# A mixture-of-experts loop on one core: pairs written out on TensorE, slot transposes between the two tiles, activated tiles copied in halves

## The chip, the cores and the metric

The kernel runs on one core of one Trainium2 chip. The metric is the device time of one execution in microseconds (us); the number that counts is the median of several executions. The core has TensorE (matrix products, transposes and the loading of their weights), VectorE, ScalarE, GpSimd and SyncE, each with its own stream of instructions; semaphores order them. PSUM is the memory into which TensorE writes, in eight banks of 512 float32 columns; SBUF is the working memory.

## The reference

A small network of six blocks on x, which is 2 x 1024 rows of 256 floats:

```python
x = x + 0.5 * moe(layernorm(x))          # 16 experts, 2 per row
x = x + attention(layernorm(x))
x = x + 0.5 * moe(layernorm(x))
x = x + 0.5 * lora(layernorm(x))         # 8 low-rank experts
x = x + latent_attention(layernorm(x))
x = x + 0.5 * lora(layernorm(x))

# moe: combine holds the softmax of the two largest router logits of a row
for e in range(NUM_EXPERTS):             # 16
    h = silu(x @ W1[e]) @ W2[e]          # 256 -> 512 -> 256
    out = out + combine[:, e:e + 1] * h
```

All is float32. The change touches the two moe blocks alone.

## The kernel before

`moe_stage` runs twice, once for each moe block. Its first part normalizes the rows, computes the router, chooses two experts for each row and sorts the 4096 pairs of row and expert by expert into tiles of 128 slots. There are at most 47 tiles (`NTILE`), each with one expert; the number of the expert of each is in `EI` in SBUF. The second part, which the change is about, takes the tiles two by two (23 pairs, `NPAIR`, and one last tile). `u` is 0 or 1, the place of a tile in its pair; every buffer has two halves, one for each.

For a tile, GpSimd gathers its 128 rows from memory into `XS` (line 675). TensorE transposes them into bank u (`slots_t`, 630, two transposes), VectorE copies that to `ST` (525). TensorE multiplies with the expert's `W1` into bank 2 + u (`hidden`, 637: two products of 512 columns, which the trace shows as four, each with its weight load). ScalarE applies silu, bank 2 + u to `HS` (552). TensorE transposes `HS` into bank 4 + u (`hidden_t`, 644, four transposes), VectorE copies the bank of 512 columns to `HT` (521). TensorE multiplies with the expert's `W2` into bank 6 + u (`expert_out`, 651: four products of 256 columns, in the trace eight). ScalarE copies the result to `YS` (556), GpSimd scatters it to memory (691).

The order on each engine is the order of the code. For pair i TensorE's is: read two expert numbers from `EI` into registers (657), `hidden` of tile 0 and 1, `hidden_t` of tile 0 and 1, `slots_t` for both tiles of the next pair, `expert_out` of tile 0 and 1. VectorE's: the two `HT` copies, the two `ST` copies. GpSimd's: two gathers, each released by a slot transpose, then two scatters, each released by a `YS` copy, then the wait for their landing (692, 693). TensorE, VectorE and ScalarE run the pairs in a loop with a register as counter (`Fori`; TensorE's at 656); the last tile, number 46, is written out behind it (666 to 669, 526 to 528, 557 to 562).

The semaphores named in the change: `s_thp` counts transposed tiles in PSUM, `s_thc` the copies of them, `s_hs` activated tiles, `s_tap` and `s_tac` transposed slots and their copies, `s_y` and `s_yc` results in PSUM and their copies. `at(n)` is the value after n of them. A wait belongs to the engine's sequencer: it holds the instructions behind it, while those already handed over go on.

Of the kernel before, what the change touches and what calls it, by code (L numbers as in the profile page):

```python
# [28 lines left out]
P = 128  # L29
# [7 lines left out]
NE, FF, TOP = 16, 512, 2  # L37
KF = FF // P

NTILE = 47  # L40
assert NTILE == NT * TOP + NE - 1
NPAIR = NTILE // 2
# [241 lines left out]
def moe_stage(nc, g, dram, rep):  # L284
# [6 lines left out]
    S = lambda name, each, **kind: g.sem("moe_" + name, each, rep, **kind)  # L291
# [12 lines left out]
    s_xs = [S(f"slots_loaded{u}", 16 * (NSLOT // 2), pool_dma=True) for u in range(2)]  # L304
    s_tap, s_tac = S("slotsT_in_psum", NSLOT), S("slotsT_copied", NSLOT)
    s_h, s_hs = S("hidden_in_psum", NTILE), S("hidden", NTILE)
    s_thp, s_thc = S("hiddenT_in_psum", NTILE), S("hiddenT_copied", NTILE)
    s_y, s_yc = S("expert_out_in_psum", NTILE), S("expert_out_copied", NTILE)
    s_yd = S("expert_out_stored", 16 * NTILE, pool_dma=True)
    s_yf = S("expert_out_free", NPAIR + 1)  # L310
# [5 lines left out]
    with ExitStack() as ctx:  # L316
# [27 lines left out]
        EC, EI = sb("EC", [1, NSLOT]), sb("EI", [1, NSLOT], I32)  # L344
# [9 lines left out]
        HT = sb("HT", [P, 2, KF, P])  # L354
        YS = sb("YS", [P, 2, D])
        bank = g.bank
# [4 lines left out]
        with nc.Block(no_gpsimd_drain=True) as block:  # L361
# [11 lines left out]
            def _(dve):  # L373
# [140 lines left out]
                for u in range(2):  # L514
                    dve.wait_ge(s_tap.handle, s_tap.at(u + 1))
                    dve.tensor_copy(ST[:, u], bank(u)[:, 0:KD * P].rearrange("p (k s) -> p k s", s=P)).then_inc(s_tac.handle, 1)  # L516
                with dve.Fori(0, NPAIR) as i:
                    for u in range(2):
                        dve.wait_ge(s_thp.handle, s_thp.at(2 * i + u + 1))
                        dve.wait_ge(s_y.handle, s_y.at(2 * i))  # L520
                        dve.tensor_copy(HT[:, u], bank(4 + u)[:, :].rearrange("p (k s) -> p k s", s=P)).then_inc(s_thc.handle, 1)  # L521
                    for u in range(2):
                        dve.wait_ge(s_tap.handle, s_tap.at(2 * i + u + 3))
                        dve.wait_ge(s_h.handle, s_h.at(2 * i + u + 1))
                        dve.tensor_copy(ST[:, u], bank(u)[:, 0:KD * P].rearrange("p (k s) -> p k s", s=P)).then_inc(s_tac.handle, 1)
                dve.wait_ge(s_thp.handle, s_thp.at(NTILE))
                dve.wait_ge(s_y.handle, s_y.at(NTILE - 1))
                dve.tensor_copy(HT[:, 0], bank(4)[:, :].rearrange("p (k s) -> p k s", s=P)).then_inc(s_thc.handle, 1)  # L528

            @block.scalar  # L530
            def _(act):
# [33 lines left out]
            def _(pe):  # L565
# [61 lines left out]
                def slots_t(u, j, loads):  # L627
                    pe.wait_ge(s_xs[u].handle, s_xs[u].at(16 * loads))
                    for k in range(KD):
                        ins = pe.transpose(bank(u)[:, k * P:(k + 1) * P], XS[:, u, k * P:(k + 1) * P], ident)  # L630
                    ins.then_inc(s_tap.handle, 1)

                def hidden(u, expert, done, j):
                    pe.wait_ge(s_tac.handle, s_tac.at(j + 1))
                    pe.wait_ge(s_hs.handle, s_hs.at(done))
                    for k in range(KD):
                        ins = pe.matmul(bank(2 + u)[:, :], ST[:, u, k, :], g.W1[:, expert, k, :], start=(k == 0), stop=(k == KD - 1))  # L637
                    ins.then_inc(s_h.handle, 1)

                def hidden_t(u, done, j):  # L640
                    pe.wait_ge(s_hs.handle, s_hs.at(j + 1))
                    pe.wait_ge(s_thc.handle, s_thc.at(done))
                    for k in range(KF):
                        ins = pe.transpose(bank(4 + u)[:, k * P:(k + 1) * P], HS[:, u, k * P:(k + 1) * P], ident)  # L644
                    ins.then_inc(s_thp.handle, 1)

                def expert_out(u, expert, done, j):
                    pe.wait_ge(s_thc.handle, s_thc.at(j + 1))
                    pe.wait_ge(s_yc.handle, s_yc.at(done))
                    for k in range(KF):  # L650
                        ins = pe.matmul(bank(6 + u)[:, 0:D], HT[:, u, k, :], W2[:, expert, k, :], start=(k == 0), stop=(k == KF - 1))  # L651
                    ins.then_inc(s_y.handle, 1)

                slots_t(0, 0, 1)
                slots_t(1, 1, 1)
                with pe.Fori(0, NPAIR) as i:
                    experts = [pe.value_load(EI[0:1, bass.ds(2 * i + u, 1)], min_val=0, max_val=NE - 1) for u in range(2)]
                    for u in range(2):
                        hidden(u, experts[u], 2 * i, 2 * i + u)
                    for u in range(2):  # L660
                        hidden_t(u, 2 * i, 2 * i + u)
                    for u in range(2):
                        slots_t(u, 2 * i + u + 2, i + 2)
                    for u in range(2):
                        expert_out(u, experts[u], 2 * i, 2 * i + u)
                expert = pe.value_load(EI[0:1, NTILE - 1:NTILE], min_val=0, max_val=NE - 1)
                hidden(0, expert, NTILE - 1, NTILE - 1)
                hidden_t(0, NTILE - 1, NTILE - 1)
                expert_out(0, expert, NTILE - 1, NTILE - 1)

            @block.gpsimd
            def _(pool):
# [1837 lines left out]
```

## Time and profile before

| | us |
|---|---|
| median of 3 runs | 2213.99 (2212.3 to 2214.46) |
| the profiled execution | 2221.23 |
| its span, from the first to the last instruction | 2219.5 |
| expert loop of the first moe block, pairs 1 to 22 | 190.72, from 81.12 |
| expert loop of the second moe block, pairs 1 to 22 | 190.71, from 797.83 |
| busy in the span: TensorE products | 1996.0 (90%) |
| VectorE | 1276.7 (58%) |
| ScalarE | 817.4 (37%) |
| GpSimd | 867.5 (39%) |

In the views PE is a product or transpose of TensorE and PEld its weight load, which runs beside the product before; DVE is VectorE, ACT ScalarE, POOL GpSimd, SP SyncE. L644 is line 644. "x4" behind a row is a number of instructions taken together, and the time ahead of it then reaches from the start of the first to the end of the last. A product's shown duration is longer than the distance at which products follow each other, since they are pipelined. In square brackets stand the idle time of the engine before the row and what ended it; "issue" means that the profile shows nothing that it waited for. A name with q (PEldq) is the engine's sequencer, which waits, branches and reads registers and is not counted as busy. [...]

### The profile page before, as it was taken

How to read it: one execution, taken by the hardware profiler on the slowest of the kernel's cores; microseconds unless marked ns; L12 is line 12 of the kernel's file. 1: busy time of each engine (PE TensorE's matmuls, PEld its weight loads, DVE VectorE, ACT ScalarE, POOL GpSimd, SP SyncE). 2: the span in 40 equal slices, each digit the busy share in tenths (PEclk: the TensorE clock that was granted, in tenths of full speed). 3: DMA queues.
4: the chain of work that ended last, by engine and by line, in shares of the span. 5: the costliest groups of instructions: out<-in, count | busy, mean ns of one | idle time of the engine just before them, and what ended most of it. 6: DMA issues, size and time to landing. Idle time of an engine off the chain costs nothing. (4 is left out here: it accounts for less than half of the span.)

```text
span 2219.5 us, 29901 instructions
## 1 busy us (share of the span) xinstructions
PE 1996.0 (90%) x8700; PEld 1249.6 (56%) x8701; DVE 1276.7 (58%) x2970; ACT 817.4 (37%) x1549; POOL 867.5 (39%) x684
## 2 busy tenths in 40 slices
PE   5899958898888789986779999999999999999987
PEld 5566635455554756654545555555566555555556
DVE  6322275777775722216656666666656666667525
ACT  2122244554555212223324444444523444444423
POOL 0344311231112034441115556555424555665631
PEclk9999968999899689996769999999999999999999
DMA  9111232232220811124141122222032222212101
GB/s 385 48 58 63 55 126 29 29 44 43 29 29 1 341 52 63 57 54 179 21 95 45 47 57 57 57 57 57 12 75 54 56 58 57 50 44 50 31 1 51
DMA packets 60570, 150.63 MB, mean 68 GB/s; under 512 B 12976, under 2 KB 18304, under 8 KB 58176
## 3 DMA queue, kind: packets, MB, share of 16 engines
q1 hardware_dynamic: 50208, 120.43, 20.6%
q0 software_dynamic: 9120, 24.92, 3.6%
q10 hardware_dynamic: 1152, 4.19, 0.5%
q8 instruction: 43, 0.70, 0.1%
q14 instruction: 47, 0.39, 0.1%
HBM read 68.95 MB, written 18.61 MB: 39 GB/s over the span
## 5 line engine op out<-in xcount | busy, mean ns | idle before, releaser
L1834 POOL TENSOR_TENSOR mla_PS<-mla_PS,mla_PT 128x1024 f32<-128x1024 f32 x192 | 458.4, 2388 | 200.2 <-ACT mla_PT L2120 198.8
L2263 DVE TENSOR_REDUCE mla_MXP<-PS 128x1 f32<-128x512 f32 x512 | 334.4, 687 | 199.7 <-PE PS L1915 197.5
L2120 ACT ACTIVATE mla_PT<-PS 128x512 f32<-128x512 f32 x512 | 293.5, 599 | 421.0 <-PE PS L1935 375.4
L1944 PE MATMUL PS<-mla_PT,mla_CN 128*64 128x512 f32 x1024 | 274.2, 614 | 0.0
L521 DVE COPY moe_HT<-PS 128x512 f32<-128x512 f32 x92 | 63.7, 692 | 307.0 <-PE PS L644 301.2
L1915 PE MATMUL PS<-mla_KH,mla_QH 113*128 113x512 f32 x512 | 199.2, 456 | 18.0 <-DMA mla_KL<-mla_SL 17.8
L675 POOL DMA_INDIRECT moe_XS<-rows_in,moe_GI x96 | 93.7, 976 | 307.5 <-PE PS L630 171.3
L1935 PE MATMUL PS<-mla_QH,mla_KH 113*128 113x512 f32 x512 | 210.3, 411 | 1.7 <-ACT mla_QH L2104 1.5
L1935 PE MATMUL PS<-mla_QL,mla_KH 113*128 113x512 f32 x512 | 201.8, 394 | 0.0
L1935 PE MATMUL PS<-mla_QH,mla_KL 113*128 113x512 f32 x512 | 201.7, 394 | 0.0
L1140 ACT ACTIVATE att_PT<-PS 128x1024 f32<-128x1024 f32 (+1 forms) x192 | 152.3, 812 | 95.2 <-PE PS L975 93.4
L1915 PEld LDWEIGHTS PS<-mla_KH,mla_QH 113*128 113x128 f32 x512 | 91.2, 194 | 168.0 <-DVE mla_MXP L2263 89.7
L637 PE MATMUL PS<-W,moe_ST 128*128 x376 | 174.4, 607 | 2.7 <-DVE moe_ST L516 2.7
L1834 POOL TENSOR_TENSOR mla_PS<-mla_PT 128x1024 f32<-128x1024 f32 x32 | 76.3, 2384 | 248.1 <-ACT mla_PT L2120 248.1
L651 PE MATMUL PS<-W,moe_HT 128*128 x752 | 170.4, 379 | 1.7 <-DVE moe_HT L528 1.7
L954 PE MATMUL PS<-att_KT,att_QT 128*128 128x512 f32 (+3 forms) x384 | 145.8, 424 | 24.4 <-DVE att_MX L1251 10.1
L651 PEld LDWEIGHTS PS<-W,moe_HT 128*128 128x128 f32 x752 | 139.1, 190 | 19.1 <-issue 2.1
L1249 DVE CUSTOM_DVE_ANT_0 PS<-PS,att_SEEN 128x128 f32<-128x128 f32 (+3 forms) x256 | 122.8, 508 | 45.8 <-PE PS L954 43.7
L852 POOL TENSOR_SCALAR_AFFINE_SELECT att_PT<-att_PT 128x256 f32<-128x256 f32 x128 | 52.2, 409 | 242.4 <-ACT att_PT L1140 242.3
L2275 DVE RECIPROCAL PS<-PS 128x128 f32<-128x128 f32 x128 | 108.7, 918 | 52.4 <-PE PS L1951 52.4
L1935 PEld LDWEIGHTS PS<-mla_QH,mla_KH 113*128 113x128 f32 x512 | 96.4, 188 | 68.3 <-issue 22.0
L954 PEld LDWEIGHTS PS<-att_KT,att_QT 128*128 128x128 f32 x384 | 74.8, 210 | 102.3 <-DVE att_MX L1251 38.5
(297 smaller groups left out, 3192.4 us busy)
## 6 DMA issues: line engine op xcount, KB each, us to landing
W<-in_W_dram SPq DMA_DIRECT2D x16, 2048.0 KB, 28.0
mla_QH<-mla_SH SPq DMA_DIRECT2D x64, 128.0 KB, 2.4
mla_KH<-mla_SH SPq DMA_DIRECT2D x64, 128.0 KB, 2.4
mla_QL<-mla_SL SPq DMA_DIRECT2D x64, 128.0 KB, 2.5
mla_KL<-mla_SL SPq DMA_DIRECT2D x64, 128.0 KB, 2.4
mla_KH<-mla_SH SPq DMA_DIRECT2D x64, 96.0 KB, 2.4
mla_KL<-mla_SL SPq DMA_DIRECT2D x64, 96.0 KB, 2.4
sums_Y<-rows_out SPq DMA_DIRECT2D x9, 512.0 KB, 6.0
```

The lines of the kernel that those rows point to most:

```text
L637: ins = pe.matmul(bank(2 + u)[:, :], ST[:, u, k, :], g.W1[:, expert, k, :], start=(k == 0), stop=(k == KD - 1))
L651: ins = pe.matmul(bank(6 + u)[:, 0:D], HT[:, u, k, :], W2[:, expert, k, :], start=(k == 0), stop=(k == KF - 1))
L954: ins = pe.matmul(out[:, m, :], QT[:, H % 2, h, i * P:(i + 1) * P], KT[:, H % 2, h // 2, k0:k0 + w], start=(m == 0), stop=(m == len(hs) - 1))
L1140: act.activation(PT[:, kk % 2, 2 * pair:2 * pair + 2, c0:HB], st_banks(s)[:, :, c0:HB], ACT.Exp, scale=SEQ ** -0.5).then_inc(s_p.handle, 1)
L1249: ins = dve.tensor_tensor_reduce(part, part, seen, 1.0, LEAST, ALU.mult, ALU.max, MX[:, q, c, h, t:t + 1])
L1834: pool.tensor_tensor(PS[:, :], PT[:, slot(0), :] if k == 1 else PS[:, :], PT[:, slot(k), :], ALU.add).then_inc(s_ps.handle, 1)
L1915: pe.matmul(bank(piece_bank(n))[:, :], QH[USED, buf, h, tile * P:(tile + 1) * P], KH[USED, buf, h, c * HB:(c + 1) * HB], start=True, stop= ...
L1935: ins = pe.matmul(bank(st_bank(s, h))[:, :], kk[USED, buf, h, ks], qq[USED, buf, h, qs], start=(n == 0), stop=(n == 2))
L1944: ins = pe.matmul(bank(6)[h * DKVL:(h + 1) * DKVL, :], CN[:, b, k, 0:DKVL], PT[:, slot(k), h * HB:(h + 1) * HB], start=(k == 0), stop=(k = ...
L2120: act.activation(PT[:, slot(k), h * HB:(h + 1) * HB], bank(st_bank(s, h))[:, :], ACT.Exp, scale=MLA_SCALE).then_inc(s_p.handle, 1)
L2263: dve.tensor_reduce(MXP[:, n // NPC, c, h, t:t + 1], bank(piece_bank(n))[:, :], AX_X, ALU.max).then_inc(s_mx.handle, 1)
L2275: dve.reciprocal(bank(A)[:, cols], bank(A)[:, cols]).then_inc(s_rc.handle, 1)
```

## The change

On VectorE the copy of an activated, transposed tile (512 columns) becomes two copies of 256 columns, each of which counts in `s_thc`, so that this semaphore now counts to 94. The order within a pair becomes: copies of tile 0, the two slot copies, copies of tile 1. On TensorE the pairs are written out in Python and no longer run in a loop. The expert numbers of the next pair are read behind `hidden` of this one, those of the first pair where they were. `slots_t` of both tiles now stands between `hidden_t` of tile 0 and `hidden_t` of tile 1. `expert_out` waits for the first half copy ahead of its first chunk and for the second ahead of its third.

```diff
--- before.py
+++ after.py
@@ -304,7 +304,7 @@
     s_xs = [S(f"slots_loaded{u}", 16 * (NSLOT // 2), pool_dma=True) for u in range(2)]
     s_tap, s_tac = S("slotsT_in_psum", NSLOT), S("slotsT_copied", NSLOT)
     s_h, s_hs = S("hidden_in_psum", NTILE), S("hidden", NTILE)
-    s_thp, s_thc = S("hiddenT_in_psum", NTILE), S("hiddenT_copied", NTILE)
+    s_thp, s_thc = S("hiddenT_in_psum", NTILE), S("hiddenT_copied", 2 * NTILE)
     s_y, s_yc = S("expert_out_in_psum", NTILE), S("expert_out_copied", NTILE)
     s_yd = S("expert_out_stored", 16 * NTILE, pool_dma=True)
     s_yf = S("expert_out_free", NPAIR + 1)
@@ -514,18 +514,22 @@
                 for u in range(2):
                     dve.wait_ge(s_tap.handle, s_tap.at(u + 1))
                     dve.tensor_copy(ST[:, u], bank(u)[:, 0:KD * P].rearrange("p (k s) -> p k s", s=P)).then_inc(s_tac.handle, 1)
+                def hidden_copy(u, done, j):
+                    dve.wait_ge(s_thp.handle, s_thp.at(j + 1))
+                    dve.wait_ge(s_y.handle, s_y.at(done))
+                    for half in range(2):
+                        part = bank(4 + u)[:, half * HALF:(half + 1) * HALF]
+                        dve.tensor_copy(HT[:, u, half * KF // 2:(half + 1) * KF // 2], part.rearrange("p (k s) -> p k s", s=P)).then_inc(s_thc.handle, 1)
+
+                HALF = KF // 2 * P
                 with dve.Fori(0, NPAIR) as i:
-                    for u in range(2):
-                        dve.wait_ge(s_thp.handle, s_thp.at(2 * i + u + 1))
-                        dve.wait_ge(s_y.handle, s_y.at(2 * i))
-                        dve.tensor_copy(HT[:, u], bank(4 + u)[:, :].rearrange("p (k s) -> p k s", s=P)).then_inc(s_thc.handle, 1)
+                    hidden_copy(0, 2 * i, 2 * i)
                     for u in range(2):
                         dve.wait_ge(s_tap.handle, s_tap.at(2 * i + u + 3))
                         dve.wait_ge(s_h.handle, s_h.at(2 * i + u + 1))
                         dve.tensor_copy(ST[:, u], bank(u)[:, 0:KD * P].rearrange("p (k s) -> p k s", s=P)).then_inc(s_tac.handle, 1)
-                dve.wait_ge(s_thp.handle, s_thp.at(NTILE))
-                dve.wait_ge(s_y.handle, s_y.at(NTILE - 1))
-                dve.tensor_copy(HT[:, 0], bank(4)[:, :].rearrange("p (k s) -> p k s", s=P)).then_inc(s_thc.handle, 1)
+                    hidden_copy(1, 2 * i, 2 * i + 1)
+                hidden_copy(0, NTILE - 1, NTILE - 1)
 
             @block.scalar
             def _(act):
@@ -639,34 +643,39 @@
 
                 def hidden_t(u, done, j):
                     pe.wait_ge(s_hs.handle, s_hs.at(j + 1))
-                    pe.wait_ge(s_thc.handle, s_thc.at(done))
+                    pe.wait_ge(s_thc.handle, s_thc.at(2 * done))
                     for k in range(KF):
                         ins = pe.transpose(bank(4 + u)[:, k * P:(k + 1) * P], HS[:, u, k * P:(k + 1) * P], ident)
                     ins.then_inc(s_thp.handle, 1)
 
                 def expert_out(u, expert, done, j):
-                    pe.wait_ge(s_thc.handle, s_thc.at(j + 1))
                     pe.wait_ge(s_yc.handle, s_yc.at(done))
                     for k in range(KF):
+                        if k % (KF // 2) == 0:
+                            pe.wait_ge(s_thc.handle, s_thc.at(2 * j + 1 + k // (KF // 2)))
                         ins = pe.matmul(bank(6 + u)[:, 0:D], HT[:, u, k, :], W2[:, expert, k, :], start=(k == 0), stop=(k == KF - 1))
                     ins.then_inc(s_y.handle, 1)
 
                 slots_t(0, 0, 1)
                 slots_t(1, 1, 1)
-                with pe.Fori(0, NPAIR) as i:
-                    experts = [pe.value_load(EI[0:1, bass.ds(2 * i + u, 1)], min_val=0, max_val=NE - 1) for u in range(2)]
+                def expert_of(j):
+                    return pe.value_load(EI[0:1, j:j + 1], min_val=0, max_val=NE - 1)
+
+                experts = [expert_of(u) for u in range(2)]
+                for i in range(NPAIR):
                     for u in range(2):
                         hidden(u, experts[u], 2 * i, 2 * i + u)
-                    for u in range(2):
-                        hidden_t(u, 2 * i, 2 * i + u)
+                    later = [expert_of(j) for j in range(2 * i + 2, min(2 * i + 4, NTILE))]
+                    hidden_t(0, 2 * i, 2 * i)
                     for u in range(2):
                         slots_t(u, 2 * i + u + 2, i + 2)
+                    hidden_t(1, 2 * i, 2 * i + 1)
                     for u in range(2):
                         expert_out(u, experts[u], 2 * i, 2 * i + u)
-                expert = pe.value_load(EI[0:1, NTILE - 1:NTILE], min_val=0, max_val=NE - 1)
-                hidden(0, expert, NTILE - 1, NTILE - 1)
+                    experts = later
+                hidden(0, experts[0], NTILE - 1, NTILE - 1)
                 hidden_t(0, NTILE - 1, NTILE - 1)
-                expert_out(0, expert, NTILE - 1, NTILE - 1)
+                expert_out(0, experts[0], NTILE - 1, NTILE - 1)
 
             @block.gpsimd
             def _(pool):
```

## Rows read from the trace of the kernel before

**Rows 1.** The page: its head and part 1.
```profile
span 2219.5 us, 29901 instructions
...
PE 1996.0 (90%) x8700; PEld 1249.6 (56%) x8701; DVE 1276.7 (58%) x2970; ACT 817.4 (37%) x1549; POOL 867.5 (39%) x684
```

**Rows 2.** Windows over pairs 1 to 22 of both stages: busy us of each engine.
```profile
81.12:271.84 190.72, 185.20 (x794) 127.73 (x793) 45.00 (x88) 42.67 (x88) 85.30 (x87) 1.00 0.20 60
797.83:988.54 190.71, 185.21 (x793) 127.73 (x792) 45.00 (x88) 42.67 (x88) 85.30 (x87) 1.00 0.19 60
```

**Rows 3.** Timeline of one pair: start, duration, engine, line, what, count, idle before.
```profile
185.15 3.60 PE L637 MATMUL PS<-W,moe_ST 128*128 x8
...
187.15 0.60 ACT L552 ACTIVATE moe_HS<-PS 128x512 f32<-128x512 f32 x1 [1.42 <-PE PS L637]
...
188.58 0.60 PE L644 MATMUL PS<-C,moe_HS 128*128 128x128 f32 x4
...
188.78 0.60 ACT L552 ACTIVATE moe_HS<-PS 128x512 f32<-128x512 f32 x1 [1.04 <-PE PS L637]
189.31 1.51 DVE L521 COPY moe_HT<-PS 128x512 f32<-128x512 f32 x2 [6.50 <-PE PS L644]
189.43 0.42 PEld L644 LDWEIGHTS PS<-C,moe_HS 128*128 128x128 f32 x4 [0.49 <-ACT moe_HS L552]
189.44 0.66 PE L644 MATMUL PS<-C,moe_HS 128*128 128x128 f32 x4 [0.25 <-ACT moe_HS L552]
...
189.93 0.60 PE L630 MATMUL PS<-C,moe_XS 128*128 128x128 f32 x4
...
190.36 3.62 PE L651 MATMUL PS<-W,moe_HT 128*128 x16
190.58 0.99 POOL L675 DMA_INDIRECT moe_XS<-rows_in,moe_GI  x1 [3.60 <-PE PS L630]
190.74 0.75 DVE L525 COPY moe_ST<-PS 128x256 f32<-128x256 f32 x2
...
193.82 3.60 PE L637 MATMUL PS<-W,moe_ST 128*128 x8
```

**Rows 4.** Waits of 80 to 270 us: us in total, times, longest.
```profile
PEld PS L644 <- ACT moe_HS L552: 10.8, 22, 0.5
```

**Rows 5.** Lines 675 (gathers), 691 (scatters) and 693 (wait for landing, 180 to 200 us).
```profile
DMA to landing us min/median/max: 2.6/2.8/4.5
...
DMA to landing us min/median/max: 2.4/2.4/3.6
...
L693 POOLq EVENT_SEMAPHORE  x2: 17/17/17, 188.4 to 197.1; - x2
```

**Rows 6.** Timeline of the first stage's last tile, where TensorE stands idle.
```profile
275.10 0.69 DVE L528 COPY moe_HT<-PS 128x512 f32<-128x512 f32 x1 [5.60 <-PE PS L644]
275.89 0.51 PEld L651 LDWEIGHTS PS<-W,moe_HT 128*128 128x128 f32 x3 [1.07 <-issue]
275.92 0.67 PE L651 MATMUL PS<-W,moe_HT 128*128 x2 [0.86 <-DVE moe_HT L528]
```

**Rows 7.** Copies of lines 521 and 525: ns least, median, most, first and last start.
```profile
L521 DVE COPY moe_HT<-PS x92: 691/692/693, 76.6 to 984.9; 128x512 f32<-128x512 f32 x92
...
L525 DVE COPY moe_ST<-PS x92: 411/415/416, 78.0 to 985.8; 128x256 f32<-128x256 f32 x92
```

**Rows 8.** TensorE's sequencer around that pair, lines 656 (whole stage), 657 and 642.
```profile
L656 PEldq COMPARE_BRANCH  x46: 83/215/238, 78.9 to 986.1; - x46
...
L657 PEldq TENSOR_LOAD <-moe_EI x2: 298/300/302, 183.2 to 183.9; - x2
L657 PEldq SEQ_ASSERT  x2: 18/18/18, 183.8 to 184.5; - x2
...
L642 PEldq EVENT_SEMAPHORE  x2: 51/51/51, 185.5 to 187.8; - x2
```

**Rows 9.** Timeline of the first stage's first pair.
```profile
68.45 0.42 DVE L516 COPY moe_ST<-PS 128x256 f32<-128x256 f32 x1 [0.73 <-PE PS L630]
...
69.87 0.50 PEld L637 LDWEIGHTS PS<-W,moe_ST 128*128 128x128 f32 x2 [1.86 <-issue]
```

**Rows 10.** The page's part 3, and the waits of the whole span.
```profile
q8 instruction: 43, 0.70, 0.1%
...
PEld PS L954 <- issue: 18.2, 31, 0.8
```

## The prediction

> **What bounds the kernel now.** I read four views, from coarse to fine. The page gives the span, 2219.5 us, and TensorE busy for 90% of it [rows 1]. [...]
>
> The timeline of one pair then shows where TensorE waits [rows 3]. Its own work is the two `hidden` groups (185.15 to 188.58), four transposes of tile 0's activations, four of tile 1's, four slot transposes, and sixteen products (190.36 to 193.82). The next pair starts when those sixteen have been issued: 16 x 0.216 = 3.46 us after 190.36, so nothing is lost at the loop's end. Four transposes take 0.43 us of issue (189.93 to 190.36). From 188.58 to 190.36 there are twelve, 1.30 us of work in 1.78 us. The missing 0.48 us lies between tile 0's transposes, issued by 188.58 + 0.43 = 189.02, and tile 1's, whose weight load starts at 189.43. The row names the releaser: the activation of tile 1 on ScalarE, 188.78 + 0.60 = 189.38. The waits view repeats it for all 22 pairs, 10.8 us on the weight-load side, 0.49 us each, and names nothing else that holds TensorE [rows 4].
>
> **The slot transposes between the tiles.** Now TensorE issues tile 0's transposes (188.58), then the slot transposes, then tile 1's. The first eight end at 188.58 + 2 x 0.43 = 189.45. Tile 1's activation still ends at 189.38, and its first weight load still starts at 189.43, as now. In stream a load starts 0.11 us before its transpose's turn, which would be 189.34, so this one is late by 0.09 and its transpose keeps the 0.06 us by which it is long now (0.66 us for four in rows 3, where four in stream take 0.60). It counts from 189.49, the four are issued by 189.93, and the products may begin there instead of at 190.36: 0.43 us gained a pair, and 0.04 us of the wait is left.
>
> Two things are moved past. The slot transposes come 0.91 us earlier than now, and they need the gathers. Gather tile 0 starts at 190.58 and lands a median of 2.8 us later [rows 5], at 193.4; its transposes stand at about 197 in the next pair, so 3 us of cover remain. On GpSimd the order is unchanged: two gathers, two scatters, a wait for their landing. That wait ends at 197.1, the gathers are released about 199.25 (190.58 + 8.67) [rows 3, 5]. With the change the gathers start at about 189.67 and the next ones 8.24 later, at 197.9; the landing moves with the products to about 196.7. 1.2 us are left where 2.15 were, enough.
>
> **The copy in halves.** This is what could take the gain away again. Products of tile 0 need its transposed activations in SBUF. The whole copy runs from 189.31 to 190.00. Then TensorE's sequencer must see it: after the last tile, where TensorE stands idle, the copy ends at 275.10 + 0.69 = 275.79 and the weight load starts at 275.89 [rows 6], 0.10 us later. Its first two products take 0.67 us, where 0.216 + 0.38 = 0.60 is the pace in stream, so they count from 275.92 + 0.08 = 276.00, 0.11 us after the load's start. So a whole copy would allow the first product at 190.00 + 0.21 = 190.21, and of the 0.43 us only 0.15 would be gained. The copy is cut into two of 256 columns each. No such copy of the hidden activations is in the trace; the nearest row is the slot copy, also PSUM to SBUF, 128x256: 0.415 us against 0.692 for 128x512 [rows 7]. The first half then ends at 189.31 + 0.415 = 189.725, the weight load may start at 189.83, the first product at 189.94. Against 189.93 from TensorE's own stream that costs 0.01 us: the two limits meet almost exactly. Bounds: none (0) to the whole copy's (0.28 us); I take 0.01 because the slot copy has the same shape, source and engine.
>
> The second half ends 0.33 us after the first (two slot copies take 0.75 in all, rows 3), at 190.06. The third chunk's product, which needs it, stands at 189.94 + 4 x 0.216 = 190.80. Behind it VectorE has the two slot copies (190.0 to 190.7) and then tile 1's halves, about 190.65 to 191.4. Tile 1's products need the first one (ready at 191.05) at 189.94 + 8 x 0.216 = 191.67: 0.6 us of cover, less 0.2 for the hand-over. The new order on VectorE, with tile 1's copy behind the slot copies, therefore costs nothing; the slot copies are needed at 193.4 only.
>
> [...]
>
> **Pairs written out, expert numbers read ahead.** Now a pair ends with a compare-and-branch (0.215 us on the sequencer) and two reads of expert numbers with their register work, first at 183.2 and done by 184.5 [rows 8]. All that lies under the sixteen products before 185.15, since the sequencer runs ahead of the array, so removing it gains 0 a pair. The reads now come after `hidden`. The sequencer is done with issuing it at 185.5 (the wait of L642) and passes the activation's wait at 187.8 [rows 8]: 2.3 us of cover for 1.3 us of reads. If that cover were gone, up to 1.3 us a pair. At the start of a stage the reads still follow the slot transposes; the slot copies are done at 68.45 + 0.42 = 68.87 and `hidden` starts at 69.87 [rows 9]. Without the loop's set-up and index arithmetic I put this 0 to 0.4 us earlier, take 0.25.
>
> **The last tile.** Everything in it is serial, and the first half copy is ready 0.692 - 0.415 = 0.28 us sooner than the whole one [rows 6, 7]. Gained: 0.28 us a stage. What follows (the last scatter, its landing, the sums) is serial too and moves with it.
>
> **The sum.** A pair gains 190.36 - 189.94 = 0.42 us, or 0.43 with the rounded starts the other way; I take 0.43. There are 23 intervals from the first `hidden` of a stage to the last tile's: 23 x 0.43 = 9.9; plus 0.28 and 0.25: 10.4 a stage, 20.9 for both. The profiled execution took 2221.23 us (span 2219.5 and 1.7 around it), 0.3% above the median of 2213.99; the gain is a matter of fixed steps, so it is taken off both: 2200.3 for a profiled run, and **2213.99 - 20.9 = 2193.1 us** for the median, 0.94% faster. A pair would last 8.24 us.
>
> **The rivals.** (a) *The half copy becomes the bound.* The two limits meet within 0.01 us, so any 0.1 us in the hand-over (a register step ahead of the weight load, a longer half copy) shows in full. With the first product 0.1 to 0.28 us late a pair gains 0.15 to 0.33: 0.33 gives 16 us (2198), 0.15 gives 8 us (2206). For it: no margin. Against it: both durations are rows. (b) *The gap isn't filled*, because slot transposes are held by something the present order hides (a gather): same time within 0.2%, about 2213. Against it: 3 us of cover. [...]
>
> **How the numbers follow.** The forecast, 0.82: by the bounds of its parts a pair gains 0.38 to 0.46 and both ends 0.3 to 0.7 a stage, 18 to 22.5 us, so 2191.5 to 2196. Rival (a) 0.12, 2196 to 2206; (b) 0.02; (c) 0.04, above 2218. With some 1.5 us for the median itself (runs went from 2212.3 to 2214.46) the range is 2190 to 2199: it reaches into (a) up to a gain of 15 us and leaves out its lower half, (b) and (c). Faster by over 0.2%: 0.82 + 0.12 = 0.94; within: 0.02; slower: 0.04.
>
> **What would show it.** A pair of 8.24 us at clock 1.00 in both loops; no idle time over 0.1 us before tile 1's weight load; the slot transposes right behind tile 0's; half copies of 0.42 us, the first ending about 0.2 us before the first product; first product 1.35 us after the pair's first transpose, now 1.78. Wrong if the products wait for the half copy (a), if idle time shows every three pairs or so (c), or if the first transposes of a pair come later than 3.43 us after its start (the reads).

## The result, and the profile after

| | before | after |
|---|---|---|
| median, us | 2213.05 | 2201.91 |
| lowest to highest of 12 runs, us | 2209.83 to 2215.53 | 2196.72 to 2208.44 |
| profiled execution, us | 2221.23 | 2202.58 |
| its span and mean granted clock | 2219.5, 0.939 | 2200.8, 0.939 |
| length of a pair, us | 8.669 | 8.348 |

The ratio is 0.9946, with an interval of 0.9936 to 0.9956: the changed kernel is faster by 0.54%, or 11.1 us in the medians (the kernel before was timed again beside it, so its median differs from the one shown ahead of the prediction). The forecast was 2193.1 us, a gain of 20.9, with a range of 2190 to 2199. The sign was right, the size half of what was said, and the time lies outside the range.

The page's head and its part 1 answer to rows 1, the row of queue 8 to rows 10. Queue 8 has 17 fetches more than before.

```profile
span 2200.8 us, 29601 instructions
...
PE 1992.3 (91%) x8700; PEld 1251.4 (57%) x8700; DVE 1277.8 (58%) x3064; ACT 817.6 (37%) x1549; POOL 866.3 (39%) x684
...
q8 instruction: 60, 0.98, 0.2%
```

The windows over pairs 1 to 22 of both stages (start:end and length, then busy us with the count of instructions in the order PE, PEld, DVE, ACT, POOL, then PEclk, which is TensorE's granted clock as a share of full speed, DMA share and GB/s; rows 2 of before):

```profile
81.22:264.87 183.65, 183.65 (x793) 128.32 (x792) 45.80 (x132) 42.70 (x88) 84.49 (x87) 1.00 0.20 62
790.80:974.46 183.66, 183.66 (x794) 128.32 (x793) 45.79 (x132) 42.69 (x88) 84.51 (x87) 1.00 0.20 63
```

183.65 / 22 = 8.348 us a pair, against 190.72 / 22 = 8.669 before, at the same granted clock (1.00 in all four windows), where 8.24 was forecast. Each of these 44 pairs lasts 8.346 to 8.349 us, so nothing happens now and then: each loses the same. TensorE counts as busy all the time, although it isn't at its pace: the product that waits is shown with 0.454 us instead of 0.379 (in stream they follow each other at 3.46 / 16 = 0.216 us, rows 3). The number to read is the length. The timeline of one pair shows the loss (rows 3 of before):

```profile
189.74 3.60 PE L641 MATMUL PS<-W,moe_ST 128*128 x8
...
193.17 0.60 PE L648 MATMUL PS<-C,moe_HS 128*128 128x128 f32 x4
193.37 0.60 ACT L556 ACTIVATE moe_HS<-PS 128x512 f32<-128x512 f32 x1 [1.04 <-PE PS L641]
193.50 0.47 PEld L634 LDWEIGHTS PS<-C,moe_XS 128*128 128x128 f32 x4
193.61 0.60 PE L634 MATMUL PS<-C,moe_XS 128*128 128x128 f32 x4
193.90 0.76 DVE L522 COPY moe_HT<-PS 128x256 f32<-128x256 f32 x2 [6.26 <-PE PS L648]
194.02 0.42 PEld L648 LDWEIGHTS PS<-C,moe_HS 128*128 128x128 f32 x4
194.04 0.63 PE L648 MATMUL PS<-C,moe_HS 128*128 128x128 f32 x4
194.27 0.99 POOL L684 DMA_INDIRECT moe_XS<-rows_in,moe_GI  x1 [2.69 <-PE PS L634]
194.53 3.32 PEld L656 LDWEIGHTS PS<-W,moe_HT 128*128 128x128 f32 x16
194.56 3.69 PE L656 MATMUL PS<-W,moe_HT 128*128 x16
194.57 0.75 DVE L530 COPY moe_ST<-PS 128x256 f32<-128x256 f32 x2
195.23 0.75 DVE L522 COPY moe_HT<-PS 128x256 f32<-128x256 f32 x2
...
197.87 0.41 PEld L641 LDWEIGHTS PS<-W,moe_ST 128*128 128x128 f32 x2
```

The order is the new one: tile 0's transposes (193.17), the slot transposes (193.61), tile 1's (194.04), with no gap between them. (Tile 1's activation still ends last by a little: 193.37 + 0.60 = 193.97, and the load of its transposes starts at 194.02, which puts them some 0.04 us behind their turn, as forecast.) The next pair starts 8.35 us after this one, at 198.09. The wait for tile 1's activation, 10.8 us in rows 4, is gone; what the waits view keeps of it is the last tile, 1.5 us once. The copy of tile 0 now comes in two halves in 0.76 us.

What remains is the start of the products. Their loads begin at 194.53. The rows of their line, and of the wait ahead of it, say why (the window is 194.2 to 194.7 us; durations are ns least, median, most, then the first and the last start; PEldq is TensorE's sequencer; the copies' row is of the whole kernel):

```profile
L522 DVE COPY moe_HT<-PS x188: 414/416/426, 77.0 to 978.1; 128x256 f32<-128x256 f32 x188
...
L655 PEldq EVENT_SEMAPHORE  x1: 51/51/51, 194.4 to 194.4; - x1
...
L656 PEldq ALU_OP  x1: 32/32/32, 194.5 to 194.5; - x1
...
L656 PE MATMUL PS<-W,moe_HT x1: 454/454/454, 194.6 to 194.6; 128*128 x1
```

The first half copy starts at 193.90 and takes 0.425 us: the 48 half copies that VectorE starts after idling take 0.424 to 0.426 us, the other 140 take 0.414 to 0.417. It ends at 194.32. The sequencer's wait on line 655 is over at 194.36, then a second instruction follows on line 656 at 194.47 (in the raw trace; the row rounds it to 194.5), and only then the load, at 194.53. The raw trace also names the semaphores: the instruction of line 655 waits for `s_thc`, the one of line 656 for `s_yc`, whose copies were done at 190.31. From the copy's end to the load it is 0.205 us, where the prediction put 0.10 by rows 6. The transposes' own stream would allow the first product at 193.17 + 1.30 + 0.05 = 194.52, where the 0.05 is mostly what tile 1's activation still costs. Counted back from its end at the pace in stream the product starts at 194.63: 0.11 us late. From the copy's end to the load it is 0.204 to 0.205 us in 45 of the 46 pairs, and 0.213 in the very first. (8.348 - 8.242) x 46 = 4.9 us; the 8.242 is measured below.

### The profile page after: what moved, and what is told of

It reads as the page before. It is cut to its first block and busy times, and to the rows that moved or that the text cites. A ratio compares the mean times of both kernels' runs of the same rounds, so it can differ in the third digit from the quotient of the medians.

```text
span 2200.8 us, 29601 instructions
## 1 busy us (share of the span) xinstructions
PE 1992.3 (91%) x8700; PEld 1251.4 (57%) x8700; DVE 1277.8 (58%) x3064; ACT 817.6 (37%) x1549; POOL 866.3 (39%) x684
## 3 DMA queue, kind: packets, MB, share of 16 engines
q1 hardware_dynamic: 50208, 120.43, 20.9%
## 5 line engine op out<-in xcount | busy, mean ns | idle before, releaser
L522 DVE COPY moe_HT<-PS 128x256 f32<-128x256 f32 x188 | 70.7, 418 | 301.5 <-PE PS L648 301.5
```

## The experiments

All kernels that follow are the changed one with the one edit shown, or the kernel before with it. Each ratio is against runs of the kernel before on the same chip.

**1. The changed kernel again.** No edit.

> The changed kernel itself, once more, beside the others on the same chip. In its profile a pair lasts 8.348 us (0.321 us less than before), which over 2 x 23 intervals is 14.8 us, and the heads and tails of the two stages give 1 us more: 15.8. The medians of the first measurement gave 11 to 12. If the missing 4 us are chance of that measurement, this one gives 14 to 17; if they are real and lie in the stages that the change doesn't touch, it gives 11 to 12 again.

Measured: 2200.92 us, ratio 0.9952 (0.9935 to 0.9968), and 8.349 us a pair. The gain is 10 to 11 us on another chip too.

**2. The two waits ahead of the products swapped.**

```diff
 def expert_out(u, expert, done, j):
-    pe.wait_ge(s_yc.handle, s_yc.at(done))
     for k in range(KF):
         if k % (KF // 2) == 0:
             pe.wait_ge(s_thc.handle, s_thc.at(2 * j + 1 + k // (KF // 2)))
+            if k == 0:
+                pe.wait_ge(s_yc.handle, s_yc.at(done))
```

> Theory: the first product of tile 0 is late because the wait for the half copy is followed by a second waiting instruction (the wait for the copied results), 0.106 us behind it on TensorE's sequencer, and by the order in which the code has them. With the two waits in the other order, the half copy's is the last and only one instruction stands between it and the weight load. Expected: first weight load of the products 0.10 to 0.11 us after the half copy's end (now 0.205), a pair of 8.24 to 8.25 us, 4.6 to 5 us less than the changed kernel in all. Rival: the half copy itself, 0.425 us and not 0.415, or the release of TensorE by VectorE takes that long whatever stands behind it: then the pair stays at 8.35 us.

Measured: 2195.20 us, ratio 0.9924 (0.9904 to 0.9945). The windows over pairs 1 to 22, the timeline of one pair, and the sequencer's rows of lines 656 and 657 in it:

```profile
80.11:261.43 181.32, 181.32 (x794) 127.90 (x792) 45.76 (x132) 42.66 (x88) 84.54 (x87) 1.00 0.20 63
```

```profile
174.20 0.60 PE L648 MATMUL PS<-C,moe_HS 128*128 128x128 f32 x4
...
174.93 0.76 DVE L522 COPY moe_HT<-PS 128x256 f32<-128x256 f32 x2 [6.16 <-PE PS L648]
175.05 0.42 PEld L648 LDWEIGHTS PS<-C,moe_HS 128*128 128x128 f32 x4
...
175.45 0.30 PEld L657 LDWEIGHTS PS<-W,moe_HT 128*128 128x128 f32 x2
```

```profile
L656 PEldq EVENT_SEMAPHORE  x1: 51/51/51, 175.1 to 175.1; - x1
...
L657 PEldq ALU_OP  x1: 32/32/32, 175.4 to 175.4; - x1
```

181.32 / 22 = 8.242 us. The half copy starts 0.73 us after the pair's first transpose as before, and ends at 175.35; the load starts at 175.45, 0.10 us later instead of 0.205, and is right behind the transposes' loads. Nothing but the order of two waits differs. In the program as written the changed kernel waits for `s_yc` first; in what TensorE runs, the wait written first comes last, on the instruction just ahead of the load, and the other on an instruction of its own before it. `s_yc` (the products of the pair before, copied out) has been reached long before (at 190.31 in the changed kernel, where the copy ends at 194.32). With `s_thc` on the earlier instruction, a wait that is already satisfied stands between the one that comes last and the load, and costs 0.106 us a pair. Swapped, the satisfied one is passed first (175.06 in the raw trace), while TensorE still works, and the one for `s_thc` (175.39) stands next to the load. The raw traces show this reversal in all the kernels compared here, the loop of the kernel before included (its source has `s_thc` first; what TensorE runs has `s_yc` at 189.56 us and `s_thc` at 190.04), but not in the loops of experiments 4 and 8. These have `s_yc` first in the source too, yet it sits on a register operation of line 655 and `s_thc` on one of line 656, next to the load, which starts 0.10 us after the copy; in the last tile of the same two kernels, which is written out, it is 0.21 us. So the order in the source alone doesn't say on which instruction a wait ends up.

**3. The pairs written out and nothing else**, in the kernel before: the loop over pairs becomes Python's, and the reads go behind `hidden`.

```diff
-with pe.Fori(0, NPAIR) as i:
-    experts = [pe.value_load(EI[0:1, bass.ds(2 * i + u, 1)], ...) for u in range(2)]
+experts = [expert_of(u) for u in range(2)]
+for i in range(NPAIR):
     for u in range(2):
         hidden(u, experts[u], 2 * i, 2 * i + u)
+    later = [expert_of(j) for j in range(2 * i + 2, min(2 * i + 4, NTILE))]
```

> The kernel before with one part of the change: pairs written out on TensorE and expert numbers read behind hidden; order and whole copies as before. By my sum a pair keeps its 8.669 us and each stage starts 0.35 to 0.4 us sooner: 2212 to 2213, ratio 0.9995 to 1.0. Rival: written-out instructions cost something outside the loops' pace (fetches, what follows the stage): then it is up to 4 us slower than before, and that is where the missing 4 us of the change went.

Measured: 2215.08 us, ratio 1.0012 (0.9998 to 1.0025), with these windows:

```profile
80.09:270.81 190.72, 185.19 (x794) 127.72 (x793) 45.00 (x88) 42.64 (x88) 85.05 (x87) 1.00 0.19 61
```

190.72 us for 22 pairs, to the hundredth what rows 2 have. By itself this part is worth nothing in the pairs. Queue 8 has 60 fetches here too, 8 of them in 81 to 271 us, where the kernel before has none; they lengthen none of these pairs.

**4. The loop kept, all else changed.**

```diff
-experts = [expert_of(u) for u in range(2)]
-for i in range(NPAIR):
+with pe.Fori(0, NPAIR) as i:
+    experts = [pe.value_load(EI[0:1, bass.ds(2 * i + u, 1)], ...) for u in range(2)]
```

> The changed kernel with TensorE's loop kept (and its reads at the head of each pair): slot transposes between the tiles and half copies only. By the sequencer's lead in the trace of before, the reads are hidden, and a pair lasts 8.35 us as in the changed kernel, perhaps up to 0.1 more since the sequencer has the reads and the branch to do ahead of the next pair. Against before: 14.8 us and the tails' 0.3, 15 us. Rival: if writing out the pairs costs 4 us outside the loops, this kernel is 3 to 4 us faster than the changed one; if it is needed for the gain, its pair is longer than 8.45 us.

Measured: 2218.99 us, ratio 1.0039 (1.0027 to 1.0052): slower than the kernel before, where a pair of 8.35 us had been expected. The windows, the timeline around a pair's end, and the rows of the sequencer there (line 656 in 183.9 to 184.4 us, line 662 in the window after it):

```profile
80.48:274.45 193.97, 186.93 (x792) 126.27 (x793) 45.78 (x132) 42.34 (x87) 84.53 (x86) 1.00 0.19 58
799.47:992.44 192.97, 186.93 (x793) 126.28 (x794) 45.78 (x132) 42.39 (x88) 84.53 (x86) 1.00 0.19 59
```

```profile
182.50 3.32 PEld L656 LDWEIGHTS PS<-W,moe_HT 128*128 128x128 f32 x16
182.60 3.63 PE L656 MATMUL PS<-W,moe_HT 128*128 x16
182.65 0.75 DVE L530 COPY moe_ST<-PS 128x256 f32<-128x256 f32 x2
183.31 0.75 DVE L522 COPY moe_HT<-PS 128x256 f32<-128x256 f32 x2
...
186.55 0.30 PEld L641 LDWEIGHTS PS<-W,moe_ST 128*128 128x128 f32 x2 [0.73 <-issue]
```

```profile
L656 PEldq ALU_OP  x1: 32/32/32, 184.1 to 184.1; - x1
...
L662 PEldq TENSOR_LOAD <-moe_EI x2: 298/299/300, 184.9 to 185.6; - x2
L662 PEldq SEQ_ASSERT  x2: 18/18/18, 185.4 to 186.2; - x2
```

193.97 / 22 = 8.817 us a pair in the first stage and 192.97 / 22 = 8.771 in the second, 0.15 and 0.10 longer than before. The sequencer can't run ahead further than the wait for tile 1's second half copy, which stands before the last two products. That copy ends at 183.31 + 0.75 = 184.06, and the wait is over at 184.10. Then come the last products' issue, the branch (0.21 us) and the two reads (0.30 us each) with their register work, done at 186.2, and the next pair's load at 186.55, 2.45 us after the wait, with 14 instructions of the sequencer in between. In experiment 2, where nothing holds it, this load starts 3.25 us after the first product (175.55 to 178.80), here that would be 182.60 + 3.25 = 185.85. It is 0.70 us late, of which 0.10 comes back because it needn't wait for its turn (from it to the next transposes it is 3.54 us instead of 3.64). The hand-over to the first product is 0.10 us in this kernel (the copy ends at 182.40, the load starts at 182.50), so 8.24 is what it starts from: 8.24 + 0.60 = 8.84, the length of this pair. The others of the first stage last 8.83 to 8.86 us and those of the second 8.79 to 8.80; the last interval of each stage, which ends with one read instead of two and no branch back, lasts 8.34.

**5. The kernel before, as the one under test.** No edit: what the comparison gives for no change.

> The kernel before, run as if it were a variant, beside the others and with a profile of its own. Four variants so far came out some 5 us later, against the kernel before, than their expert stages explain: the traces give 15.6, 21, 2 and -2.6 us for these stages, the medians gave 10.6, 16.3, -3.6 and -7.5. If that is real and lies in the untouched stages, this run gives a ratio of 1.000. If it comes from how the kernel before is run among the others, it gives 1.002 (5 us) for the same code. Its profile shows whether the attention and latent-attention stages last 435 and 1132 us, as in the variants, or less.

Measured: 2214.21 us, ratio 1.0003 (0.9991 to 1.0014), 8.669 us a pair.

**6. The copy left whole**, in the changed kernel.

```diff
-for half in range(2):
-    part = bank(4 + u)[:, half * HALF:(half + 1) * HALF]
-    dve.tensor_copy(HT[:, u, half * KF // 2:(half + 1) * KF // 2], part.rearrange(...)).then_inc(s_thc.handle, 1)
+dve.tensor_copy(HT[:, u], bank(4 + u)[:, :].rearrange(...)).then_inc(s_thc.handle, 1)
```

With it `s_thc` counts to 47 again, and `expert_out` waits for it once, behind `s_yc` in the source as in the changed kernel.

> The changed kernel with the activated tile copied whole (512 columns), everything else as changed. By the prediction's sum the first product then starts 0.692 + 0.205 us after the copy's start, 0.27 us later than in the changed kernel, where the half copy takes 0.425: a pair of 8.62 us, some 12 us slower than the changed kernel in all. Rival: if the copy isn't what the first product waits for, the pair stays at 8.35 us.

Measured: 2214.31 us, ratio 1.0002 (0.9991 to 1.0012), with these windows:

```profile
81.29:270.81 189.52, 186.35 (x793) 128.32 (x792) 42.92 (x88) 42.69 (x88) 84.48 (x87) 1.00 0.19 60
```

189.52 / 22 = 8.615 us, where 8.62 had been expected. Without the halves the new order on TensorE is worth 0.054 us a pair, and nothing that the median shows. The halves carry 0.27 of the 0.32 us.

**7. The best of what the runs point to:** the waits swapped as in 2, and the first pair's expert numbers read ahead of the first slot transposes, so that TensorE waits with them for a gather that it has to wait for anyway.

```diff
-slots_t(0, 0, 1)
-slots_t(1, 1, 1)
 def expert_of(j):
     return pe.value_load(EI[0:1, j:j + 1], min_val=0, max_val=NE - 1)
 experts = [expert_of(u) for u in range(2)]
+slots_t(0, 0, 1)
+slots_t(1, 1, 1)
```

> The changed kernel with the two waits swapped, and with the first pair's expert numbers read ahead of the first slot transposes instead of behind them. A pair of 8.242 us as with the waits swapped alone. The reads take 1.3 to 1.6 us of TensorE's sequencer where it waits for a gather anyway, so each stage's first hidden follows its slot copies after 0.2 us instead of 0.6 to 0.9: about 1 us in all less than with the waits swapped. Against before: the expert stages give 22 us; with the 4 to 5 us that all variants so far lost elsewhere, 17 to 18 us in the medians.

Measured: 2191.61 us, ratio 0.9901 (0.9885 to 0.9917). It beats both kernels: 22 us less than the one before beside it, where the changed one was 11 us less. Its windows, and the first stage's first pair:

```profile
77.92:259.24 181.32, 181.32 (x793) 127.91 (x792) 45.75 (x132) 42.66 (x88) 84.56 (x87) 1.00 0.20 63
```

```profile
67.48 0.42 DVE L516 COPY moe_ST<-PS 128x256 f32<-128x256 f32 x1 [0.92 <-PE PS L634]
...
68.14 0.55 PEld L641 LDWEIGHTS PS<-W,moe_ST 128*128 128x128 f32 x2
...
68.60 0.42 DVE L516 COPY moe_ST<-PS 128x256 f32<-128x256 f32 x1 [0.69 <-PE PS L634]
```

The copy at 67.48 is that of tile 0's slots, the only one that tile 0's `hidden` needs. It ends at 67.91, and `hidden` loads 0.24 us later, right behind tile 1's slot transposes; tile 1's copy starts only at 68.60. The same copy in the kernel before, and in the changed kernel with the first load of `hidden`:

```profile
67.29 0.42 DVE L516 COPY moe_ST<-PS 128x256 f32<-128x256 f32 x1 [0.89 <-PE PS L630]
```

```profile
68.01 0.42 DVE L516 COPY moe_ST<-PS 128x256 f32<-128x256 f32 x1 [0.93 <-PE PS L634]
...
70.16 0.50 PEld L641 LDWEIGHTS PS<-W,moe_ST 128*128 128x128 f32 x2 [1.44 <-issue]
```

From the copy's end to the load it was 69.87 - 67.71 = 2.16 us before (the load is in rows 9), and it is 70.16 - 68.44 = 1.72 us in the changed kernel: the loop's set-up is gone, the two reads are still there. Rows 9 show tile 1's copy, which ends at 68.87; it is not what `hidden` waited for, the reads are.

The edit is worth more than the 1 us that was expected. Against experiment 2 the two stages are 1.9 and 2.4 us shorter: 1.2 and 1.0 between the first gather and the first `hidden`, and 0.7 and 1.5 in the first interval, which lasts 9.56 and 9.84 us here and 10.27 and 11.31 there. The first interval of the same code varies by up to 0.75 us from trace to trace (the last section), so that second part may be luck in part. By the medians the kernel gains 22 us, where 17 to 18 were expected.

**8. The loop kept, and VectorE's order of before:** kernel 4 with both tiles' half copies ahead of the slot copies.

```diff
-hidden_copy(0, 2 * i, 2 * i)
+for u in range(2):
+    hidden_copy(u, 2 * i, 2 * i + u)
 for u in range(2):
     ...
-hidden_copy(1, 2 * i, 2 * i + 1)
```

> TensorE's loop kept, slot transposes between the tiles, half copies, but on VectorE the order of before: both tiles' activated copies, then the slot copies. Theory: with the loop kept and the new order on VectorE a pair took 8.84 us because the wait for tile 1's second half copy (over at 184.06 us of that trace) holds the sequencer, and behind it still stand the branch and both reads (2.4 us) before hidden can be issued, 0.49 us too late. In the old order tile 1's copies end 0.46 us sooner, so hidden is 0 to 0.05 us late: a pair of 8.24 to 8.29 us, as good as written out. Rival: the branch and the reads cost 0.5 us a pair in themselves, once the gap between the tiles no longer absorbs them: then the pair stays at 8.7 to 8.85 us.

Measured: 2198.34 us, ratio 0.9938 (0.9922 to 0.9954), with these windows, the sequencer's row of line 656 (169.1 to 169.5 us), and the load of the pair after it:

```profile
80.10:263.50 183.40, 183.40 (x794) 126.26 (x793) 47.82 (x132) 42.67 (x88) 84.45 (x87) 1.00 0.19 62
```

```profile
L656 PEldq ALU_OP  x1: 32/32/32, 169.3 to 169.3; - x1
```

```profile
171.79 0.30 PEld L641 LDWEIGHTS PS<-W,moe_ST 128*128 128x128 f32 x2 [0.23 <-issue]
```

183.40 / 22 = 8.336 us, and 8.345 in the second stage, between the expectation (8.24 to 8.29) and the rival. From the wait for the last half copy to the next pair's load it is 2.45 us again (169.34 to 171.79), but the wait is over sooner, and the load comes 0.20 us late instead of 0.70; with 0.10 of it regained, 8.24 + 0.10 = 8.34. Experiments 3, 4 and 8 together: taking the branch out and moving the reads behind `hidden` gains 0.00 us a pair in the kernel before, and what they cost at a pair's end in the other two, where the sequencer takes 2.45 us from the last wait to the next load, goes with where VectorE's last half copy ends. The written-out pairs are needed above all by the new order on VectorE, where the loop costs 0.55 to 0.60 us a pair. With VectorE's old order it still costs 0.09 to 0.10 (8.336 and 8.345 against 8.242), about what the order of the waits costs the changed kernel. Written-out pairs with VectorE's old order weren't run.

**9. The kernel before with 48 satisfied waits** put on TensorE at the start of each stage, where it stands idle for a gather: does a mere shift of the code change the rest?

```diff
 pe.wait_ge(s_ei.handle, s_ei.at(1))
+for _ in range(48):
+    pe.wait_ge(s_ei.handle, s_ei.at(1))
```

> The kernel before with 48 waits that are satisfied already (2.4 us of TensorE's sequencer) where TensorE waits for the first gather, in both stages. A pair keeps 8.669 us. All later instructions of TensorE stand 48 instructions further on for each stage, which is what all variants have in common. If the 4 to 5 us that they lost come from where TensorE's instructions lie, this kernel is 3 to 5 us slower than before too; if not, the ratio is 1.000 within 0.1%.

Measured: 2215.63 us, ratio 1.0012 (0.9999 to 1.0026), 8.669 us a pair.

**10. The kernel before once more**, beside 9.

> The kernel before as a variant once more, on the chip of the three others: its ratio says how much of a difference of 1 to 2 us means nothing. Expected 1.000 within 0.1%. Its trace is the third of before: the latent-attention stage took 1137.7 and 1137.2 us in the first two and 1131.6 to 1134.8 in four of the five variants, although the medians say that before is the one with less time there.

Measured: 2215.09 us, ratio 1.0011 (1.0001 to 1.0022). So 9 shows nothing that no edit at all doesn't show, and neither does 3. A ratio of 1.001 is not a difference here, even where its interval leaves out 1.

## Why the prediction went wrong, point by point

**What bounds the kernel, the wait that goes, the slot transposes: right.** The twelve transposes stand in stream, the wait for the activation is gone and no gather holds the slot transposes (the gather at 194.27 here starts 0.06 us after they end). Once the wait order is mended a pair lasts 8.242 us, where 8.24 was said.

**The failed step: the hand-over to the first product, put at 0.10 us by rows 6.** It measured 0.205 in the changed kernel and 0.10 in experiments 2, 4 and 8. The row was right for what it shows: there the order in the source was `s_thc`, then `s_yc`, so the copy's wait sat on the instruction next to the load. The diff turns this order round in `expert_out`, and the prediction took no account of it. The half copy also took 0.425 us instead of 0.415. With a margin of 0.01 us the hand-over shows in full: 0.321 a pair instead of 0.43. Swapping the waits gives 0.106 of the missing 0.109 back, which leaves 0.003 for the longer half copy and all else. 46 x 0.109 = 5.0 us of the 9.8 that are missing in the median; another 0.5 us is missing at the ends of the stages and 4.3 us outside them, as the passages below work out. It is rival (a), and its condition was named (a register step ahead of the weight load), but at 0.12 it was given too little: where two limits meet within 0.01 us, a forecast by either one needs every instruction between them to be counted, and I counted none.

**The whole copy: right in kind, mis-sized by the same term.** 0.15 us of gain were to remain by the hand-over of 0.10; experiment 6 has 0.054. It too has the waits in the new order, and its load starts 0.205 us after the copy's end, 0.105 later than was put: 0.15 - 0.105 = 0.045. The whole copy with the waits swapped wasn't run.

**The half copies: 0.415 us by the row of the slot copies, right within 0.011.** All 188 half copies take 0.414 to 0.426 us. A second instruction has a price of its own: two halves take 0.75 to 0.76 us where one whole copy took 0.692 (rows 7), so it costs 0.06 us in a row. The time was lost behind the copy and not in it.

**"The new order on VectorE costs nothing" and "removing the branch and the reads gains 0": right in the sum, wrong one by one.** I priced each edit against the kernel before. Written out alone it is 0 (experiment 3). But the new order ends tile 1's copy later and takes from the sequencer the lead under which the branch and the reads had lain; at the same hand-over writing out is now worth 0.60 us a pair in the first stage (8.84 in experiment 4 against 8.24 in 2) and 0.55 in the second. In the prediction that copy's cover was counted for TensorE's array, 0.6 us, and not for the sequencer's work behind its wait. The reads after `hidden` are hidden, as forecast.

**The ends of a stage.** From the stage's first gather to its last scatter the changed kernel is 7.8 us shorter in the first stage and 7.5 in the second, where 10.4 were forecast. 22 pairs give 7.07. From the first gather to the first `hidden` it is 0.41 and 0.35 us less (forecast 0.25). The last tile gives 0.16 (forecast 0.28): its half copy is ready 0.28 sooner, and the doubled hand-over takes 0.11 back. The first interval, from the first `hidden` to the second pair's, gives 0.20 and -0.04 us where 0.43 was put, for a reason that the sum hadn't: TensorE's first products stand 0.85 us apart there instead of 0.43, for a time that varies, as the last section shows. For the two stages it makes 15.4 us.

**What is missing outside the stages.** The sum took the rest of the kernel as unchanged. The traces account for 15.4 us in the two stages, and the medians differ by 11.1. A single pair of traces can't say where the other 4.3 us are: the two profiled executions differ by 18.7 us (2219.5 and 2200.8), because the one of before was 8 us above its median. The same comparison, mean difference in time less the difference in the stages, leaves 4.2 us in the first measurement, 4.9 in experiment 1, 4.0 in 2, 4.9 in 3, 3.0 in 4, 4.4 in 6, 3.4 in 7 and 1.0 in 8; for the kernel before against itself 0.6 and 2.4, and 4.2 for the padded one. The means have an uncertainty of about 1.1 us, and the stages of one trace another of 1 us or so, since their first intervals vary (the last section). So the average of the controls is 1.5 us with no edit, that of the changed kernels 3.7, and some 2 us are left, hardly more than the uncertainty. Divided another way, the six kernels whose pairs are written out average 4.3 us (3.4 to 4.9) and the five others 2.2 (0.6 to 4.2), so a price of some 2 us for the written-out code outside the pairs is neither shown nor excluded. The mean granted clock moves with the time: it is 0.9419 over the 70 runs of before beside the experiments and 0.9390 over the 12 of the changed kernel. As an estimate, with all of the missing share taken as time at a granted 0.50 (twice that share of the span), it is 257 and 268 us; among the runs of before, a microsecond more of this goes with 0.29 us more time, so these 11 us would stand for 3.3. That is a correlation. Padding TensorE's code (experiment 9) didn't tell this apart from the control, and no run here shows what would lower the mean clock. It stays open.

**Fetching the written-out code, rival (c): not so in the pairs.** Rival (c), with its 0.04 above 2218 us, was that fetching the written-out pairs makes the kernel slower. Queue 8 has 60 fetches where it had 43, of 16 KB each (0.98 and 0.70 MB). In pairs 1 to 22 there are 8 in each stage of the changed kernel (81 to 265 and 790 to 975 us) and none in either stage of the kernel before (81 to 272 and 797 to 989); experiments 4 and 8, which keep the loop, have 43 fetches as before. None of the changed kernel's 44 pairs is longer than 8.349 us. No run shows a fetch that stops TensorE, nor idle time every three pairs or so, and so none shows the term that a time above 2218 us would need; a price of 2 us outside the pairs is not excluded, as said above.

## What to carry to other kernels

When an edit makes two limits meet, count every instruction of the sequencer between the releaser and the released one, waits that are long satisfied included (one cost 0.106 us a pair here); put the wait that comes last last in what the engine runs (in the written-out code here: first in the source; in the loops of experiments 4 and 8 it was last there), and read in the trace on which instruction it ended up. Price an edit in the kernel with the other edits in it: here the branch and the two register reads at a pair's end cost 0.00 us in the old order (experiment 3) and 0.55 to 0.60 in the new one (experiments 2 and 4). Count the sequencer's lead from the last wait that it had to pass, 2.45 us ahead of the next load in experiments 4 and 8, and not from where the array is. Where an interval leaves out 1 by 0.1%, time the kernel before against itself before believing it.

## What was unexpected of the hardware

A satisfied wait between the one that comes last and the load costs 0.106 us a pair. The hand-over is 0.204 to 0.213 us in all 46 pairs of the changed kernel and 0.100 to 0.108 us in all 46 of experiment 2.

With two register reads and a branch in between, the sequencer takes 2.4 to 2.5 us from the last wait to the next load in nearly every pair of experiments 4 and 8 (2.58 in the first), although the reads themselves take 0.30 us each and the branch 0.21.

When a stage starts, TensorE's first products stand 0.85 us apart instead of 0.43, for a time that varies from one execution to the next. In the second stage the granted clock is lower for that time. These are windows around the start of the second stage's first `hidden` (at 786.48 before and 779.42 after), in the columns of rows 2:

```profile
785.00:789.00 4.00, 2.76 (x5) 1.18 (x4) 0.42 (x1) 0.00 (x0) 1.32 (x2) 0.50 0.24 66
789.00:793.00 4.00, 4.00 (x10) 1.71 (x8) 0.00 (x0) 0.80 (x2) 0.00 (x0) 0.66 0.00 0
```

```profile
779.00:783.00 4.00, 3.58 (x5) 1.52 (x6) 0.07 (x1) 0.00 (x0) 0.82 (x1) 0.50 0.25 70
783.00:787.00 4.00, 4.00 (x15) 2.20 (x14) 0.39 (x2) 1.20 (x2) 0.00 (x0) 0.71 0.00 0
```

The granted clock is 0.50 there while TensorE waits for the gathers and when the first `hidden` begins. In windows of 1 us it still is in 790 to 791 us before and in 784 to 785 after, and it is 1.00 from 792 and from 786 on, within the first pair. In the first stage the granted clock reads 1.00 in all of 66 to 78 us of both kernels, and yet the loads of the first `hidden` stand 0.85 us apart there too (70.89, 71.74 and 72.59 us before; 71.17, 72.03 and 72.88 after), so the clock on record doesn't explain it there. The first interval lasts 11.25 and 11.35 us in the profiled execution of before, 11.05 and 11.39 in that of after, against 8.67 and 8.35 for a later pair. It varies: the kernel before has 11.64 and 11.29 us in experiment 5 and 11.13 and 10.60 in experiment 10, the changed one 10.60 and 11.32 in experiment 1. The others have 10.21 and 10.74 (experiment 3, whose later pairs are those of before), 10.27 and 11.31 (experiment 2), and 9.56 and 9.84 (experiment 7, whose `hidden` starts soonest). What sets the length of this time isn't shown here. The stages of one trace can therefore differ by 1 us with no cause in the edit, and a fair reading of a change goes by the later pairs.
